# The four narrow maxima of an item ahead of its values

## The chip, the cores and the metric

The kernel runs on one core of a Trainium2 chip. The metric is device time in microseconds (us) of one launch, from the first to the last instruction of the program and what lies around them. Before the change it is 5533.32 us, the median of three runs (5531.68 to 5542.09).

## The reference

Eight samples of 256 channels x 32 x 32 in float32 go through four layers, each a kind of attention over the 1024 tokens of a sample. Cut to what matters here:

```python
# L0, L2: 8 heads of 32 channels        L1: the same 8 heads, and two more of 128 channels
xn = group_norm(x); q, k, v = split(qkv_w @ xn + qkv_b)
weight = softmax((q * s).T @ (k * s))          # [1024, 1024] for each sample and head
h = weight @ v                                  # then the projection, its bias and the residual
# L1 also: position added, a small 3x3 convolution whose sigmoid scales x, both attentions
#          concatenated, silu(... @ ff_w1) @ ff_w2 @ out_w, group norm, residual
# L3: one head of 256 channels
```

So each sample has three narrow attentions (8 heads of 32 channels; layers 0, 1 and 2) and two wide ones (two heads of 128 channels in layer 1, one of 256 in layer 3). The softmax subtracts the maximum of a row of scores. What is computed for that: an approximate score matrix once with tokens of q in partitions, whose row maxima are taken, and the exact scores a second time, transposed, with the negative maximum added inside the matmul as a 97th row.

## The kernel before, in words

**Samples and slots.** Attentions of two samples alternate: while one sample's attention runs, the work between two attentions of the other (projections, norms, convolution) is laid into its loop. `turns` makes these slots, `stages` gives each piece of between-work a place in units, and `plan` writes one list of events, PLAN, which every engine walks in the same order. Nothing is scheduled at run time: each engine executes its own instructions strictly in that order and waits on semaphores.

**Units, items, steps.** A narrow attention (kinds "0", "1", "2") has 128 units u. One unit is one score tile: 128 keys x 512 queries of one head. Four units, the four heads of a group at the same keys, are an item; 8 items are a step (one group of heads and one half of the queries), and there are 4 steps. In each unit PE issues `score`, then `rest` of the attention before (its tail), then `rest` of this one, then the between-work that is due.

**What a unit's pieces are.** ACT takes the exponential of each score tile into the ring PR of three items (L836). `values_narrow` (L562), at u = 6, 10, 14, ..., multiplies the probabilities of the item whose last score was u-3 with the values: eight matmul instructions in four column groups of 32, and their four results side by side in one bank, held over the step. `sums_narrow` (L577) does the same with ones, for the softmax's denominators: of the items 6 and 7 of a step directly (u % 32 = 2 and 4), and of the others after POOL has added their probabilities (L1133, L1120), at u % 32 = 6. `quad` (L626) is four approximate score matmuls of four heads for the *next* step, in four row groups of 32, one PSUM bank each; VectorE takes the row maxima of the four (L943), one in each of the units u to u+3. `quads_at` (L291) puts quads of steps 1 to 3 at every fourth unit from `first_quad` (L286), that is u = 2, 6, ..., 82; the first eight quads of an attention, and three of step 1, are issued by the between-work ahead of it. When all maxima of a step are there, `columns` turns them on PE, and a DMA lays them into the 97th row.

**Banks.** PSUM has 8 banks. `take` (L507) gives the bank that is not held and was given back longest ago, and makes PE wait until the engine that read its last content has read it. A score's bank goes to the back of that order at once; the banks of a quad are held and given back one per unit (`maximum`, `give`); the values' and the sums' banks are held for longer. In `quad` all four banks are taken, with their waits, before its first matmul.

In `rest` (L646), at a unit where both stand, PE therefore issues: the last part of the sums if due, the values, the first or second part of the sums if due, then the quad, then `maximum` (for a narrow attention it only gives a bank back).

Of the kernel before, what the change touches and what calls it, by code (L numbers as in the profile page):

```python
# [285 lines left out]
def first_quad(s):  # L286

    return 32 * (s - 1) - 4 * EARLY_QUADS + 2


def quads_at(att, u):  # L291

    if not att.wide:
        for s in range(1, att.steps):
            n, r = divmod(u - first_quad(s), 4)
            if r == 0 and 0 <= n < QUADS and (s > 1 or n >= EARLY_QUADS):
                return s, n
    return None


def maxima_at(att, u):

    out = []
    if u < att.units:
        for s in range(1, att.steps):
            first = 2 * (u - att.per * (s - 1)) if att.wide else u - first_quad(s)
            for p in range(first, first + (2 if att.wide else 1)):
                if 0 <= p < att.maxima and not (s == 1 and not att.wide and p < GROUP * EARLY_QUADS):
                    out.append((s, p))
    return out  # L310
# [14 lines left out]
def after_step(att, u, what):  # L325

    off = ((13, 14, 14, 15, 16) if att.wide else (38, 39, 40, 41, 43))[what]
    s, r = divmod(u - off, att.per)
    return s if r == 0 and 0 <= s < att.steps else None


def items_at(att, u):

    if att.wide:
        return [(s, kt) for s in range(att.steps) for kt in range(8) if u == att.per * s + max(4, kt + 3)]
    return [(s, i) for s in range(att.steps) for i in range(8) if u == att.per * s + 4 * i + 6]
# [21 lines left out]
def build_program(nc, x, pos, resident, stream, fold, out):  # L358
    ctx = ExitStack()
    with ctx:  # L360
# [115 lines left out]
        def until_read(eng, key):  # L476
            bank, n, _ = tiles[key]
            eng.wait_ge(read[bank], n + 1)
# [5 lines left out]
        def filling(key):  # L484
            return full[tiles[key][0]]

        def half(nh):
            return slice(nh * HALF, (nh + 1) * HALF)
# [11 lines left out]
        def _(pe):  # L500
            def mm(dst, lhsT, rhs, start, stop, **kw):
                return nc.tensor.matmul(dst, lhsT, rhs, start=start, stop=stop, **kw)  # L502
# [4 lines left out]
            def take(key, hold=False, says_full=True):  # L507

                bank = min((i for i in range(BANKS) if i not in held.values()), key=lambda i: (given[i], i))
                tiles[key] = bank, uses[bank], fulls[bank]  # L510
                if uses[bank]:
                    pe.wait_ge(read[bank], uses[bank])
                uses[bank] += 1
                fulls[bank] += says_full
                count["turn"] += 1
                given[bank] = count["turn"]
                if hold:
                    held[key] = bank
                return PS[bank]
# [33 lines left out]
            def sums(bank, probs, start, stop):  # L553
                for j in range(GROUP):
                    ins = mm(bank[D * j:D * j + D, :], ONES[:, 0:D], probs[:, j, :], start, stop,
                             tile_position=(0, D * j))
                return ins

            def narrow_probs(att, s, i):
                return PR[:, (att.item0 + 8 * s + i) % P_RING, :, :]  # L560
# [16 lines left out]
            def sums_narrow(att, s, part):  # L577
                key = ("sums", att.index, s)
                if part < 2:
                    if part == 0:  # L580
                        take(key, True)
                    sums(PS[tiles[key][0]], narrow_probs(att, s, ADDED + part), part == 0, False).then_inc(p_used, 1)
                else:
                    pe.wait_ge(p_added, att.adds0 + att.adds * (s + 1))
                    sums(PS[tiles[key][0]], ADD, False, True).then_inc(filling(key), 1)

            def values_wide(att, s, kt):
                until_read(pe, ("score", att.index, 8 * s + kt))
                keys = [("av", att.index, s), ("av2", att.index, s)][:att.ctiles]
                probs = PR[:, (att.item0 + 2 * s + kt // 4) % P_RING, kt % 4, :]  # L590
                for d, key in enumerate(keys):

                    if kt == 0:
                        take(key, True, d + 1 < att.ctiles)
                    col = (att.head(s) + d) * P
                    ins = mm(PS[tiles[key][0]][:, :], VT[:, att.index % 2, kt, col:col + P], probs, kt == 0, kt == 7)
                    if kt == 7 and d + 1 < att.ctiles:
                        ins.then_inc(filling(key), 1)
                if kt % 4 == 3:
                    ins.then_inc(p_used, 1)  # L600

            def sums_wide(att, s):
                key = ("sums", att.index, s)
                bank = take(key, True)
                pe.wait_ge(p_added, att.adds0 + att.adds * (s + 1))
                mm(bank[:, :], ONES[:, :], ADD[:, 0, :], True, True).then_inc(filling(key), 1)

            def maximum(att, s, p):
                key = ("max", att.index, s, p)
                if not att.wide:  # L610

                    give(key)
                    return
                bank = take(key)
                if s == 0 and p == 0:
                    until_read(pe, ("q", att.index, (1, 1)))
                    until_read(pe, ("k", att.index, (1, 1)))
                q, k = (wide_part(att.kind, o, "hi") for o in "qk")
                qt, kh = divmod(p, NH)
                q0 = s % NH * HALF + qt * P  # L620
                for ct in range(att.ctiles):
                    g = att.head(s) + ct
                    ins = mm(bank[:, :], q[:, g, q0:q0 + P], k[:, g, half(kh)], ct == 0, ct == att.ctiles - 1)
                ins.then_inc(filling(key), 1)

            def quad(att, s, n):  # L626
                g = s // NH
                if n == 0:
                    until_read(pe, ("k", att.index, (g, 1)))
                    until_read(pe, ("q", att.index, (g, s % NH)))  # L630
                qt, kh = divmod(n, NH)
                q0 = s % NH * HALF + qt * P
                keys = [("max", att.index, s, GROUP * n + j) for j in range(GROUP)]
                banks = [take(key, True) for key in keys]
                for j, key in enumerate(keys):
                    r = slice(D * j, D * j + D)
                    mm(banks[j][:, :], HIS[r, g, 0, q0:q0 + P], HIS[r, g, 1, half(kh)], True, True,
                       tile_position=(D * j, 0)).then_inc(filling(key), 1)
# [7 lines left out]
            def rest(att, u):  # L646
                if att.wide:
                    for s, p in maxima_at(att, u):
                        maximum(att, s, p)
                s = after_step(att, u, SUMMED)  # L650
                if s is not None and att.wide:
                    sums_wide(att, s)
                elif s is not None:
                    sums_narrow(att, s, 2)
                for s, i in items_at(att, u):
                    if att.wide:
                        values_wide(att, s, i)
                    else:
                        values_narrow(att, s, i)
                if not att.wide and u >= 34 and u % 32 in (2, 4) and u < att.units + 5:  # L660
                    sums_narrow(att, u // 32 - 1, (u % 32 - 2) // 2)
                four = quads_at(att, u)
                if four is not None:
                    quad(att, *four)
                if not att.wide:
                    for s, p in maxima_at(att, u):
                        maximum(att, s, p)
                s = columns_at(att, u)
                if s is not None:
                    columns(att, s)  # L670

                s = after_step(att, u, TURNED)
                if s is not None:
                    give(("sums", att.index, s))
                s = after_step(att, u, NORMED)
                if s is not None:
                    for name in ("av", "av2")[:att.ctiles]:
                        give((name, att.index, s))
# [46 lines left out]
            for event, it, i in PLAN:  # L725
# [74 lines left out]
                elif event == "v":  # L800
                    four, part = i
# [576 lines left out]
```

## Time and profile before

| | |
|---|---|
| median of three runs | 5533.32 us |
| profiled execution, its own time | 5545.02 us |
| its span, first to last instruction | 5543.2 us |
| mean granted TensorE clock | 0.933 |
| busy: PE matmul, PE weight load | 91%, 41% |
| busy: DVE, ACT, POOL | 51%, 50%, 58% |
| chain that ended last | PE 63%, DVE 9%, issue 9%, ACT 9%, POOL 8% |

PE is TensorE's matmuls, PEld its weight loads, DVE VectorE, ACT ScalarE, POOL GpSimd. A busy share is an average over stretches with different limits, and the chain of waits says which engine the end hung on, step by step. Instructions are named by the source line and by tile: out<-in. Nearly all matmuls are recorded under one helper line, L502, so the tile names tell them apart: `q_stack,k_stack` with 97 rows is a narrow score, `high_parts` with 32*128 a quad, `probs,v_tokens` with 128*32 narrow values, `probs,ones` and `probs_added,ones` sums.

### The profile page before, as it was taken

The page shows a single profiled execution, that of the slowest core. Times are in us where ns is not written, and L with a number is a line of the kernel's source. Part 1 is how long each engine was busy: PE and PEld are TensorE (multiplying, and loading weights), DVE is VectorE, ACT ScalarE, POOL GpSimd, SP SyncE. Part 2 cuts the span into 40 slices and gives each one's busy share as a digit, 9 for nine tenths or more (in the row PEclk, how much of TensorE's full clock was granted, in tenths as well). Part 3 has the DMA queues.
Part 4 walks back from the last instruction along what each step waited for, and adds up shares of the span by engine and source line. Part 5 has one row for each costly group of instructions (what it writes and reads, how often), then busy time and mean ns, then how long its engine had stood idle before and what let it go on. Part 6 is the DMA issues. An engine that isn't in the chain of part 4 may idle for free.

```text
span 5543.2 us, 63206 instructions
## 1 busy us (share of the span) xinstructions
PE 5032.5 (91%) x22016; PEld 2259.8 (41%) x22016; DVE 2851.5 (51%) x5110; ACT 2752.0 (50%) x4738; POOL 3232.3 (58%) x1777
## 2 busy tenths in 40 slices
PE   7788989999899998999999999999999999899887
PEld 3235333543335433354334543345333453334534
DVE  5345656256553565535655366544566346563362
ACT  3353665345663456524565255652556525555252
POOL 4474667546674476735767357664576636666363
PEclk8899889999899998999989999999899999899999
DMA  2112111022110211102210112101122012120020
GB/s 83 29 29 58 45 45 37 20 58 53 38 30 27 63 48 31 33 21 63 54 40 19 36 49 54 46 12 40 45 54 51 8 44 55 40 52 7 17 49 12
DMA packets 103609, 221.20 MB, mean 40 GB/s; under 512 B 31105, under 2 KB 33409, under 8 KB 103169
## 3 DMA queue, kind: packets, MB, share of 16 engines
q1 hardware_dynamic: 103296, 217.16, 15.1%
q8 instruction: 181, 2.97, 0.2%
q14 instruction: 132, 1.07, 0.1%
HBM read 56.47 MB, written 8.39 MB: 12 GB/s over the span
## 4 chain that ended last, share of the span: by engine, by line
PE 63%; DVE 9%; issue 9%; ACT 9%; POOL 8%; SPq 1%; DMA 1%; POOLq 0%; ACTq 0%; DVEq 0%
PE bank L502 63%; DVE max_cols L943 6%; POOL probs_added L1133 4%; ACT probs L836 3%; POOL probs_added L1120 3%; ACT L836 1%; ACT act L846 1%; DVE dev_squared L1054 1%; DVE stats L1040 1%; ACT act L855 1%; DVE sums_turned L965 1%; SPq L1220 0%; ACT L877 0%; SPq L1209 0%; DVE sums_turned L973 0%
## 5 line engine op out<-in xcount | busy, mean ns | idle before, releaser
L943 DVE TENSOR_REDUCE max_cols<-bank 128x1 f32<-128x512 f32 x3456 | 2183.8, 681 | 1822.3 <-PE bank L502 1818.5
L836 ACT ACTIVATE probs<-bank 128x512 f32<-128x512 f32 x3456 | 1921.2, 599 | 2267.2 <-PE bank L502 2131.4
L1133 POOL TENSOR_TENSOR probs_added<-probs_added,probs 128x1024 f32<-128x1024 f32 x768 | 1801.2, 2369 | 196.4 <-ACT probs L836 195.8
L502 PE MATMUL bank<-q_stack,k_stack 97*128 97x512 f32 (+1 forms) x3584 | 1669.6, 523 | 129.5 <-DVE max_cols L943 66.2
L502 PE MATMUL bank<-probs,v_tokens 128*32 128x512 f32 (+1 forms) x7168 | 1400.0, 649 | 44.1 <-ACT probs L836 44.1
L502 PEld LDWEIGHTS bank<-q_stack,k_stack 97*128 97x128 f32 (+1 forms) x3584 | 666.4, 197 | 891.5 <-issue 461.3
L502 PE MATMUL bank<-act,weight_stream 128*128 128x512 f32 x1792 | 952.8, 632 | 34.2 <-issue 8.3
L1133 POOL TENSOR_TENSOR probs_added<-probs 128x1024 f32<-128x1024 f32 x192 | 452.6, 2369 | 708.8 <-PE bank L502 682.1
L1120 POOL TENSOR_TENSOR probs_added<-probs 128x512 f32<-128x512 f32 x48 | 60.9, 1269 | 883.8 <-PE bank L502 851.9
L502 PE MATMUL bank<-high_parts 32*128 32x512 f32 x3072 | 409.6, 521 | 144.0 <-ACT probs L836 73.6
L502 PEld LDWEIGHTS bank<-probs,v_tokens 128*32 128x32 f32 (+1 forms) x7168 | 329.8, 123 | 515.2 <-issue 362.1
L502 PEld LDWEIGHTS bank<-high_parts 32*128 32x128 f32 x3072 | 160.3, 191 | 830.2 <-issue 752.2
L502 PEld LDWEIGHTS bank<-act,weight_stream 128*128 128x128 f32 x1792 | 327.8, 196 | 344.2 <-issue 278.2
L1120 POOL TENSOR_TENSOR probs_added<-probs_added,probs 128x512 f32<-128x512 f32 x288 | 373.0, 1295 | 57.5 <-ACT probs L836 32.0
L502 PE MATMUL bank<-k_stack 128*128 128x512 f32 x512 | 273.7, 573 | 53.0 <-ACT probs L836 36.2
L1172 POOL TENSOR_TENSOR low_parts<-full_parts,high_parts 128x512 fp32r<-128x512 f32 x192 | 243.9, 1274 | 100.0 <-ACT full_parts L909 100.0
L502 PE MATMUL bank<-weight_stream,act 128*128 128x256 f32 x1024 | 268.4, 391 | 0.0
L965 DVE STREAM_TRANSPOSE sums_turned<-bank 128x512 f32<-128x512 f32 x144 | 101.8, 707 | 321.1 <-PE bank L502 321.0
L502 PE MATMUL bank<-probs,ones 128*32 128x512 f32 x1536 | 225.1, 662 | 0.0
L502 PEld LDWEIGHTS bank<-weight_stream,act 128*128 128x128 f32 x1024 | 189.3, 192 | 71.1 <-issue 48.6
L955 DVE CAST neg_max_t<-bank 16x128 fp32r<-16x128 f32 (+1 forms) x144 | 39.7, 275 | 337.2 <-PE bank L644 337.2
L846 ACT ACTIVATE act<-act,gn_shift,gn_scale 128x512 f32<-128x512 f32 x192 | 148.3, 805 | 126.5 <-DVE gn_shift L1069 126.5
(82 smaller groups left out, 3479.5 us busy)
## 6 DMA issues: line engine op xcount, KB each, us to landing
k_stack<-high_parts SPq DMA_DIRECT2D x384, 128.0 KB, 2.4
q_stack<-high_parts SPq DMA_DIRECT2D x768, 64.0 KB, 2.0
weight_stream<-stream_dram SPq DMA_DIRECT2D x32, 768.0 KB, 4.4
k_stack<-low_parts SPq DMA_DIRECT2D x192, 128.0 KB, 2.4
q_stack<-low_parts SPq DMA_DIRECT2D x384, 64.0 KB, 2.0
act<-x_dram SPq DMA_DIRECT2D x8, 1024.0 KB, 6.5
act<-pos_dram SPq DMA_DIRECT2D x8, 1024.0 KB, 6.0
weight_stream<-stream_dram SPq DMA_DIRECT2D x16, 512.0 KB, 3.7
```

The lines of the kernel that those rows point to most:

```text
L502: return nc.tensor.matmul(dst, lhsT, rhs, start=start, stop=stop, **kw)
L836: act.activation(PR[:, m % P_RING, j, :], bank[:, :], ACT.Exp, scale=att.scale).then_inc(reading(key), 1)
L846: act.activation(act_buf(it.turn, dst)[:, t, half(nh)], act_buf(it.turn, src)[:, t, half(nh)], ACT.Identity, scale=GA[:, t:t + 1], bias=GS ...
L855: ins = act.activation(padded_image(it.turn)[D * j:D * j + D, 1 + rows * i:1 + rows * (i + 1), 2 - j:2 - j + SIDE], bank[D * j:D * j + D, ...
L943: dve.tensor_reduce(cols[:, kh, j, qt:qt + 1], bank[:, :], AX.X, ALU.max).then_inc(reading(key), 1)
L955: dve.tensor_copy(NT_[0:att.cols, :], bank[0:att.cols, 0:P]).then_inc(reading(key), 1)
L965: dve.transpose(RT[:, :], bank[:, :]).then_inc(reading(key), 1)
L1040: mark("stats", dve.bn_stats(ST[:, t, nh, :], act_buf(it.turn, src)[:, t, half(nh)]))
L1054: dve.tensor_tensor(SQ[:, :], DV[:, :], DV[:, :], ALU.mult).then_inc(gn_dev, 1)
L1120: pool.tensor_tensor(ADD[:, 0, :], one, two, ALU.add).then_inc(p_added, 1)
L1133: pool.tensor_tensor(ADD[:, js, :], one, two, ALU.add).then_inc(p_added, 1)
L1172: pool.tensor_tensor(low, whole, high.bitcast(F32), ALU.subtract).then_inc(lo_ready, 1)
```

## The change

In PE's `rest` the quad is issued ahead of the values (and ahead of the first and second part of the sums) instead of behind them. The `maximum` calls that give the banks back stay where they were, behind everything. No other engine's code changes. Since banks are handed out in PE's order, a quad that stands at a unit where values or sums take a bank now takes its four first.

```diff
@@ -652,6 +652,9 @@
                     sums_wide(att, s)
                 elif s is not None:
                     sums_narrow(att, s, 2)
+                four = quads_at(att, u)
+                if four is not None:
+                    quad(att, *four)
                 for s, i in items_at(att, u):
                     if att.wide:
                         values_wide(att, s, i)
@@ -659,9 +662,6 @@
                         values_narrow(att, s, i)
                 if not att.wide and u >= 34 and u % 32 in (2, 4) and u < att.units + 5:
                     sums_narrow(att, u // 32 - 1, (u % 32 - 2) // 2)
-                four = quads_at(att, u)
-                if four is not None:
-                    quad(att, *four)
                 if not att.wide:
                     for s, p in maxima_at(att, u):
                         maximum(att, s, p)
```

## Rows read from the trace of the kernel before

**Rows 1.** The page, busy us (share of the span) xinstructions:
```profile
PE 5032.5 (91%) x22016; PEld 2259.8 (41%) x22016; DVE 2851.5 (51%) x5110; ACT 2752.0 (50%) x4738; POOL 3232.3 (58%) x1777
```

**Rows 2.** Waits, whole span; engine waited <- releaser: us, times, longest us:
```profile
DVE max_cols L943 <- PE bank L502: 1818.5, 760, 27.7
...
PEld bank L502 <- ACT probs L836: 319.0, 523, 3.7
PEld bank L502 <- DVE max_cols L943: 311.4, 569, 3.8
...
PE bank L502 <- ACT probs L836: 205.0, 213, 4.1
...
PE bank L502 <- DVE max_cols L943: 142.1, 270, 3.3
...
PE bank L502 <- DVE mean_var L1045: 25.2, 12, 8.6
```

**Rows 3.** PE and PEld by shape: busy, mean ns | idle before <-releasers:
```profile
L502 PE MATMUL bank<-q_stack,k_stack 97*128 97x512 f32 x3072 | 1466.7, 544 | 129.5 <-DVE max_cols L943 66.2 <-ACT probs L836 34.4 <-DVE group_mean L1055 18.5
...
L502 PE MATMUL bank<-probs,v_tokens 128*32 128x512 f32 x6144 | 893.1, 656 | 44.1 <-ACT probs L836 44.1
...
L502 PE MATMUL bank<-high_parts 32*128 32x512 f32 x3072 | 409.6, 521 | 144.0 <-ACT probs L836 73.6 <-DVE max_cols L943 55.4 <-ACT full_parts L909 12.7
...
L502 PEld LDWEIGHTS bank<-q_stack,k_stack 97*128 97x128 f32 x3072 | 568.6, 198 | 847.0 <-issue 429.7 <-DVE max_cols L943 225.9 <-ACT probs L836 105.9
```

**Rows 4.** Windows: stretch: length, PE, PEld, DVE, ACT, POOL busy (x), PEclk, DMA, GB/s:
```profile
2897.50:3042.20 144.70, 136.20 (x693) 57.28 (x694) 79.66 (x141) 83.66 (x153) 104.78 (x50) 0.96 0.12 32
2551.60:2719.90 168.30, 154.18 (x714) 62.20 (x713) 101.47 (x181) 101.75 (x172) 116.76 (x60) 0.92 0.20 51
2719.90:2897.50 177.60, 160.03 (x729) 57.98 (x729) 102.35 (x185) 107.42 (x179) 115.42 (x60) 0.88 0.17 42
...
308.20:337.10 28.90, 26.77 (x161) 8.97 (x153) 22.06 (x38) 17.06 (x32) 23.38 (x10) 0.97 0.09 22
```

**Rows 5.** Timeline, laden turn at 2954 us; start, length, engine, line, op:
```profile
2954.09 0.82 PE L502 MATMUL bank<-q_stack,k_stack 97*128 97x512 f32 x2
2954.71 1.09 ACT L836 ACTIVATE probs<-bank 128x512 f32<-128x512 f32 x2 [0.42 <-PE bank L502]
...
2954.84 1.07 PE L502 MATMUL bank<-probs,v_tokens 128*32 128x512 f32 x8
...
2955.83 0.50 PE L502 MATMUL bank<-high_parts 32*128 32x512 f32 x4
...
2956.27 1.13 PE L502 MATMUL bank<-wv_wp,act 128*128 128x256 f32 x4
```

**Rows 6.** Timeline, the same attention's first and last moved turn:
```profile
2905.84 1.09 ACT L836 ACTIVATE probs<-bank 128x512 f32<-128x512 f32 x2 [1.63 <-PE bank L502]
...
2906.85 1.04 PE L502 MATMUL bank<-probs,v_tokens 128*32 128x512 f32 x8
...
2994.05 1.57 ACT L836 ACTIVATE probs<-bank 128x512 f32<-128x512 f32 x3 [0.71 <-PE bank L502]
...
2995.13 1.06 PE L502 MATMUL bank<-probs,v_tokens 128*32 128x512 f32 x8
```

**Rows 7.** Timeline, a score's weight load that waits for a maximum:
```profile
2909.10 0.19 PEld L502 LDWEIGHTS bank<-q_stack,k_stack 97*128 97x128 f32 x1 [0.66 <-DVE max_cols L943]
```

**Rows 8.** Timeline, a turn with nothing laid between, at 323 us:
```profile
323.79 0.51 PE L502 MATMUL bank<-high_parts 32*128 32x512 f32 x4
...
324.23 1.34 PE L502 MATMUL bank<-q_stack,k_stack 97*128 97x512 f32 x4
324.32 2.48 DVE L943 TENSOR_REDUCE max_cols<-bank 128x1 f32<-128x512 f32 x4 [0.23 <-PE bank L502]
324.77 2.07 ACT L836 ACTIVATE probs<-bank 128x512 f32<-128x512 f32 x4 [0.61 <-PE bank L502]
...
326.50 0.50 PE L502 MATMUL bank<-high_parts 32*128 32x512 f32 x4
```

## The prediction

> **What bounds the kernel now.** I read the shares first, then the waits, then the shapes on TensorE, then single turns. TensorE (PE) is busy for 91% of the span [rows 1]. The waits say that the other engines mostly wait for PE: the maxima on VectorE stood idle 1818 us for it. PE itself waited for the exponentials of ScalarE and for the maxima of VectorE, some hundreds of microseconds in four rows [rows 2]. So PE sets the pace; it is an in-order engine that stalls locally, and the change reorders exactly such a place. The shapes show what is reordered: 768 groups of four narrow maxima (a "quad") and 768 items of values [rows 3].
>
> Two kinds of stretch must be told apart. Of the 24 narrow attentions, 21 run beside another sample's projections and norms ("laden"): 145 to 178 us each. Three run with little beside them: the step of 28.9 us there has GpSimd busy 23.4 us, with additions for five of the eight items, so GpSimd's run and the turn to the next one set it [rows 4].
>
> **How many turns change.** Quads of steps 1 to 3 stand in the narrow loop at u = 2, 6, ... 82; that at u = 2 has no values beside it. That leaves 20 of an attention, 480 in all (420 laden, 60 not). The other 288 are issued by the between-work or at u = 2 and stay. DVE's, ACT's, POOL's and SP's orders are untouched, and no DMA moves. At u = 34 and 66 the quad is also moved past the first part of the sums; at u = 38 and 70 the last part stays ahead of it.
>
> **The engine's own time for the order.** A turn of now: two scores at 2954.09, values at 2954.84, quad at 2955.83, next work at 2956.27: values cost 0.99 us, the quad 0.44 [rows 5]. After: score, quad, values, score, the same pieces with the same number of changes between them. The pairs score-quad and quad-values are not in the trace. The nearest rows bound them: from the first of two scores to the values behind them it is 0.75 us, change and all, and a quad is left in 0.44 [rows 5]. I allow 0.1 us either way per turn, 480 x 0.1 = 48 us both ways, and take zero, except for u = 38 and 70, where sums and values no longer stand together: 48 turns x 0.1 = 5 us more.
> The trace shows values left only after 0.99 us although the quad, with a single pass, is left after 0.44 [rows 5]. The Trainium skill (TensorEngine Tiling (Array Packing), Key Properties) says that changing the tiling mode drains the engine. By that rule there are three drains in a turn before and after, four instead of three in the 48 turns named; by it the sum would gain the same few microseconds.
>
> **New stall ahead of the quad (the main term).** The quad takes four banks at once, the four free longest, and waits for the reader of each. By the rule of the banks (seven or fewer are free, each score and each given maximum goes to the back) the newest of the four was last used by the score one turn of the loop back (u-1) in about three of four quads, and by u-2 in the rest. The exponential of that score has not been taken when score u is issued. Now the values stand in between and hide it: at 2954.84 the values start; the two exponentials from 2954.71 take 1.09 us, so the first ends at 2955.26, and the quad, 0.2 later, could start at 2955.46. Now it starts at 2955.83 with no stall; after the change PE stands 2955.46 - 2954.84 = 0.62 us with the ready values queued behind it [rows 5]. In the first moved quad of that attention the first of the two exponentials from 2905.84 ended at 2906.39, before the values' 2906.85: nothing. In the last the exponentials end at 2995.62 and the values start at 2995.13: 0.63 us [rows 6]. The same subtraction, less whatever stall that turn has already, over all 20 turns of this attention (these are its first, its eleventh and its last) gives 0, 0.89, 0, 0.62, 1.00, 0.86, 0.41, 0.96, 0, 0, 0.61, 0, 0.95, 0.64, 0.86, 0.61, 0.51, 1.00, 0.62, 0.64: sum 11.2 us, 0.56 per turn. Bounds: 0, and 0.99 per turn (all the cover), 480 x 0.99 = 475 us. For 21 laden attentions: 21 x 11.2 = 235 us.
>
> Who is held up by the later values themselves? ACT, which needs their slot in the ring for the score at u+6, over an item later, and the sums behind them; neither is late by 1 us. The wait of a step's first quad for its q and k goes ahead of the values too (u = 22, 54), and those copies are long made.
>
> **What comes back.** First, where the newest bank waits for a maximum of the quad before, that maximum is itself earlier, since its own quad went ahead of its values: of the 11.2 us 2.6 vanish so. Second, scores now wait for banks whose maximum is not read, as 0.66 us at 2909.10 [rows 7], and for exponentials; with the quad up to a microsecond earlier relative to the scores, and ACT caught up during PE's stall, these shrink. Score waits in weight loads and matmuls sum to 226 + 106 + 66 + 34 = 432 us [rows 3]; the share of the moved turns is 480/768, 270 us, the upper bound (the lower is zero). Following each turn's own score waits I take 3.0 us of an attention, 63 for 21. Third, a delay that reaches a place where PE waits for a chain of a norm or of a projection's copy anyway is lost there; such waits are single rows of some 25 us [rows 2], and I take 40 us in all. Laden sum: 235 - 21 x 2.6 - 63 - 40 = 77 us.
> In the three lightly laden attentions the loop is another: quad 323.79, maxima from 324.32 for 2.48 us, next quad 326.50: VectorE's loop of 2.71 us [rows 8]. After, the loop goes quad 0.44, values 0.99, scores, the second or third exponential (1.6 to 2.1 us after the first score), 0.2: 3.2 to 3.7 us. But this falls in items that GpSimd's run mostly hides; what is left is about one turn per step, 9 x 0.6 = 5 us, and I take 8.
>
> Sum: 77 + 8 + 5 = 90 us. Profiled execution: 5545.0 us, of which span 5543.2; 5545 + 90 = 5635, 1.62% more. On the median of 5533.3: 5623; I say 5620.
>
> **Rivals.**
> (1) The early maxima win (faster). VectorE starts 0.4 to 1.0 us earlier, so scores no longer wait for its banks: 226 + 66 = 292 us of waits on maxima [rows 3], 5/8 of it 183; if the exponentials mostly are in time, so that the new stall is under some 0.2 us per turn, it is under 96 us and 5533 - 70 = about 5465 follows. For it: VectorE's idle time for PE, and turns as the first of rows 6. Against: rows 5 is the common turn. It decides when net new stall passes the score waits returned, about 0.25 us per turn.
> (2) Absorbed. If other waits take all that is added, as GpSimd does in the light steps [rows 4], the time stays within 11 us. Against: the laden steps wait little for GpSimd.
> (3) The clock gives a second price. The granted clock was 0.96 in the attention with the fewest stalls and 0.92 and 0.88 in the others, with PE's busy share 94, 92 and 90% [rows 4]: the lower level, 1.2 of 2.4 GHz, is granted more where PE stalls more. If the change costs 0.04 of the clock in 21 attentions with 150 us of busy PE each, that is 150 x 0.04/0.92 x 21 = 137 us on top of some 80: about 5750. The Trainium skill (TensorE: Matmul & The Clock Gate, section "A second HAM failure mode: psum-queue depth-cycling") says that short idles between groups of matmuls while PSUM banks are cycled make the clock oscillate; the rows here lean that way, but the laden attentions with long chains of a norm have the low clock too, so short stalls are not shown to be its cause.
> (4) That the edit does nothing is excluded: in 480 turns instructions of PE change places.
>
> **Numbers.** Forecast case 0.60 (its own range 5560 to 5690: the new stall between 0.4 and 0.75 us per turn, drains either way); clock 0.14; absorbed 0.07; faster 0.19. Faster and slower mean by over 0.2%, 11 us, about what a measurement of this kernel can tell from no change. The slower side is 0.60 + 0.14 = 0.74. The range 5500 to 5730 leaves out the better half of rival 1 and the far end of rival 3.
>
> **What would show it.** Right: the idle of PE before the quads' matmuls (144.0 us, of it 73.6 for exponentials [rows 3]) rises by 100 us or more and is now for the exponentials; values directly behind a quad with no wait of their own; maxima start nearer to the last score; score waits on maxima fall below 226 us; a common laden turn is longer by 0.3 to 0.6 us; the wide attentions keep their times. Wrong: if quads wait for nothing in most turns, the bank argument falls; if pairs score-quad and quad-values together cost 0.2 us more or less than 0.8, the drains do; if the clock moves by more than 0.01, rival 3 has a share.

## The result

The changed kernel takes 5667.0 us (median of 4 runs, 5663.7 to 5669.9) against 5537.7 us before on the same chip (4 runs): ratio 1.023, 95% interval 1.0214 to 1.0246, slower by some 127 us. The profiled execution's span is 5661.9 us, 118.7 us more than before, at a mean granted clock of 0.934 (before 0.933). Forecast were 5620 and a ratio of 1.016: the direction and the mechanism held; the slowdown is 1.4 times what was said (127 against 90 us).

The page of the kernel after, shares; PE is busy 41 us less in a span 119 us longer [rows 1]:

```profile
PE 4991.7 (88%) x22016; PEld 2265.0 (40%) x22016; DVE 2868.1 (51%) x5110; ACT 2745.9 (48%) x4738; POOL 3232.6 (57%) x1777
```

Its waits over the whole span, in the columns of [rows 2]:

```profile
DVE max_cols L943 <- PE bank L502: 1876.2, 762, 27.7
...
PEld bank L502 <- ACT probs L836: 443.5, 616, 3.7
PE bank L502 <- ACT probs L836: 401.5, 454, 5.1
...
PEld bank L502 <- DVE max_cols L943: 173.1, 291, 2.1
...
PE bank L502 <- DVE max_cols L943: 81.5, 114, 2.0
```

PE's waits for exponentials rose from 524 to 845 us, those for maxima fell from 454 to 255 us. A weight load and its matmul can show one wait twice, so these figures give directions and must not be added up.

PE (matmuls) and PEld (weight loads) by shape, answering to [rows 3]:

```profile
L502 PE MATMUL bank<-q_stack,k_stack 97*128 97x512 f32 x3072 | 1443.4, 541 | 84.9 <-ACT probs L836 37.5 <-DVE max_cols L943 26.9 <-DVE group_mean L1055 13.9
...
L502 PE MATMUL bank<-probs,v_tokens 128*32 128x512 f32 x6144 | 896.8, 658 | 34.4 <-ACT probs L836 34.4
...
L502 PE MATMUL bank<-high_parts 32*128 32x512 f32 x3072 | 411.0, 520 | 363.9 <-ACT probs L836 266.0 <-DVE max_cols L943 47.0 <-ACT full_parts L909 33.0
...
L502 PEld LDWEIGHTS bank<-q_stack,k_stack 97*128 97x128 f32 x3072 | 571.3, 200 | 954.9 <-issue 631.3 <-ACT probs L836 152.6 <-DVE max_cols L943 104.1
```

The quads are where the time went: PE's idle time before their matmuls rose from 144.0 to 363.9 us, and the part of it that an exponential ended rose from 73.6 to 266.0 us. The scores got something back: idle before their matmuls 129.5 -> 84.9, and their weight loads' waits for maxima 225.9 -> 104.1 us; but their waits for exponentials grew (105.9 -> 152.6).

The three kinds of laden attentions, in the columns of [rows 4]. The lines show the changed kernel: kind 0, kind 2, kind 1.

```profile
2607.20:2784.40 177.20, 157.39 (x714) 63.50 (x713) 100.56 (x181) 101.71 (x172) 116.71 (x60) 0.89 0.19 48
2784.40:2961.80 177.40, 152.12 (x729) 57.34 (x729) 103.26 (x185) 107.22 (x179) 115.50 (x60) 0.91 0.17 42
2961.80:3115.50 153.70, 139.60 (x692) 58.81 (x693) 80.46 (x141) 83.47 (x153) 104.85 (x50) 0.93 0.12 30
```

In these three, kind 0 went from 168.3 to 177.2 us, kind 2 from 177.6 to 177.4 and kind 1 from 144.7 to 153.7 (the last is the largest growth of its kind). Averaged over the seven of each, from the first exponential of an attention to that of the next, the growth is 10.0, 1.0 and 5.1 us; the three lightly laden ones grew by 7.7 us together, the wide ones shrank by 1.5 us together. All of it arises in steps 0 to 2; step 3, without moved quads, is the same within 0.4 us.

The turn of [rows 5], the eleventh moved one of that attention, in the changed kernel:

```profile
3018.02 0.81 PE L502 MATMUL bank<-q_stack,k_stack 97*128 97x512 f32 x2
3018.64 1.09 ACT L836 ACTIVATE probs<-bank 128x512 f32<-128x512 f32 x2 [0.42 <-PE bank L502]
...
3019.38 0.51 PE L502 MATMUL bank<-high_parts 32*128 32x512 f32 x4 [0.55 <-ACT probs L836]
...
3019.82 1.07 PE L502 MATMUL bank<-probs,v_tokens 128*32 128x512 f32 x8
```

Before, it was 0.75 us from the first of the two scores to the values, then 0.99 to the quad and 0.44 to the next work. Now it is 1.36 us from score to quad and 0.44 from there to the values. The quad waited until just after the first exponential ended (3018.64 + 0.55 = 3019.19, and 0.19 more), as was worked out for it. The new stall is 1.36 - 0.75 = 0.61 us.

### The profile page after: what moved, and what is told of

Its sections match the earlier page's. It is cut to its first block, busy times and chain, and to the rows that moved or that the text cites. A ratio compares the mean times of both kernels' runs of the same rounds, so it can differ in the third digit from the quotient of the medians.

```text
span 5661.9 us, 63206 instructions
## 1 busy us (share of the span) xinstructions
PE 4991.7 (88%) x22016; PEld 2265.0 (40%) x22016; DVE 2868.1 (51%) x5110; ACT 2745.9 (48%) x4738; POOL 3232.6 (57%) x1777
## 4 chain that ended last, share of the span: by engine, by line
PE 63%; ACT 12%; issue 9%; DVE 8%; POOL 6%; SPq 1%; DMA 1%; POOLq 0%; DVEq 0%; ACTq 0%
PE bank L502 63%; ACT probs L836 6%; DVE max_cols L943 4%; POOL probs_added L1120 3%; POOL probs_added L1133 3%; ACT L836 1%; DVE dev_squared L1054 1%; ACT act L846 1%; ACT full_parts L909 1%; ACT act L855 1%; ACT L877 1%; SPq L1220 0%; DVE stats L1040 0%; SPq L1209 0%; ACT high_parts L908 0%
## 5 line engine op out<-in xcount | busy, mean ns | idle before, releaser
L502 PE MATMUL bank<-q_stack,k_stack 97*128 97x512 f32 (+1 forms) x3584 | 1646.5, 520 | 84.9 <-ACT probs L836 37.5
L502 PE MATMUL bank<-high_parts 32*128 32x512 f32 x3072 | 411.0, 520 | 363.9 <-ACT probs L836 266.0
L502 PE MATMUL bank<-q_stack 128*128 128x512 f32 x512 | 203.9, 455 | 3.6 <-DMA neg_row<-neg_max_t 2.1
```

## The experiments

All are small edits to one of the two kernels. Times are medians, and each ratio is to the kernel before, measured beside that run. Its median moved between 5527.9 and 5541.9 us from one set of runs to the next, so small differences are read from ratios. The changed kernel's own time is 5667.0 us. Lines left out of an edit are marked " ...".

**1. Fill the stall.** If PE stands idle between score and quad, work put there is free. The filler is two matmuls of the shape of a score, 0.46 us in all, whose result is overwritten.

```diff
+            def filler(att, u, s, n):
+                key = ("max", att.index, s, GROUP * n)
+                bank, now = take(key, True), u // att.per
+                for _ in range(2):
+                    mm(bank[:, :], KS[0:97, GROUP * att.head(now), 0:P], QS[0:97, att.buf(now), 0, :], True, True)
 ...
                 four = quads_at(att, u)
+                if four is not None and u >= 6:
+                    filler(att, u, *four)
 ...
```

> The changed kernel with two idle score-like matmuls (0.46 us, result overwritten) into the quad's own oldest bank, after the score and ahead of the quad's other three waits, in all 480 moved turns: 221 us of added PE work. Theory (PE stands there anyway in 352 turns): most of it is swallowed by the stall, +40 to +110 us: 5705 to 5775. Rival (the loss is engine time of the order, not a wait): all is added, 5870 or more.

> The kernel before with the same two idle matmuls behind the score, ahead of the values. There the wait for the values' exponential swallows some 60 us of the 221: 5660 to 5740. Theory: the distance between the two kernels shrinks from 127 us to 0 to 80; rival: it stays 100 to 150.

Measured: the changed kernel with fillers took 5666.4 us, without them 5667.0: 480 fillers, 221 us of matmuls, added nothing. The kernel before with fillers took 5611.6 us against 5541.9, ratio 1.013 (1.0102 to 1.0158). The two filled kernels stand 55 us apart, the plain ones 125 to 129. Both times are below what was expected; the distance lies in the range of the theory. The quads' row by shape, of the changed kernel with fillers, then of the kernel before with fillers:

```profile
L502 PE MATMUL bank<-high_parts 32*128 32x512 f32 x3072 | 408.3, 517 | 134.3 <-ACT probs L844 36.8 <-DVE max_cols L951 31.1 <-issue 26.5
```

```profile
L502 PE MATMUL bank<-high_parts 32*128 32x512 f32 x3072 | 399.8, 509 | 52.6 <-DVE max_cols L951 25.1 <-ACT probs L844 18.5 <-ACT full_parts L917 7.2
```

The idle time before the quads falls by 230 us in the changed kernel (363.9 to 134.3), as much as was filled in, and by 91 us in the kernel before (144.0 to 52.6). So most of the loss is time in which PE stands between score and quad, not time that PE needs for another order. The run times alone would not show this, because the clock rose too, to 0.945 (changed, filled) and 0.955 (before, filled). An estimate: two runs of the kernel with short exponentials below, 5406.4 us at 0.941 and 5384.3 at 0.949, differ by 2.8 us for each 0.001 of the clock. By that the clock gave back some 30 and 60 us, and some 190 of the 221 us were hidden in the changed kernel, some 90 in the one before.

**2. Shorten what is waited for.** Each exponential is taken over a quarter of its columns; the other three quarters are left out of the computation.

```diff
-                act.activation(PR[:, m % P_RING, j, :], bank[:, :], ACT.Exp, scale=att.scale).then_inc(reading(key), 1)
+                act.activation(PR[:, m % P_RING, j, 0:P], bank[:, 0:P], ACT.Exp, scale=att.scale)\
+                   .then_inc(reading(key), 1)
 ...
```

> The kernel before, with each exponential taken over 128 of the 512 columns (the others hold ones and are left out of the computation). It is the base for the next run. PE waited 524 us for exponentials in all; some of it goes: 5250 to 5500.

> The changed kernel with the same short exponentials (three quarters of each left out). Theory (quads ahead of the values wait for the exponential of the score before last): that exponential is now there some 0.3 us sooner and ACT has no backlog, so the 127 us between the two kernels shrink to 30 to 80 us (what stays is the change from score to quad, 0.42 against 0.32 us, and part of the latency of PE and ACT). Rival (the order itself costs on PE): the distance stays 110 to 140 us.

Measured: 5385.9 and 5507.3 us, 121 us apart. The expectation of 30 to 80 was missed, and the rival's number of 110 to 140 was met. The changed kernel with short exponentials, by shape:

```profile
L502 PE MATMUL bank<-high_parts 32*128 32x512 f32 x3072 | 415.7, 526 | 288.1 <-ACT probs L837 141.3 <-DVE max_cols L945 102.3 <-ACT full_parts L911 22.6
```

and the kernel before with them:

```profile
L502 PE MATMUL bank<-high_parts 32*128 32x512 f32 x3072 | 411.3, 523 | 120.6 <-DVE max_cols L945 61.1 <-ACT probs L837 47.6 <-ACT full_parts L911 6.9
```

The rival's number need not have the rival's cause, because the stall before quads is still there: 288 against 121 us, 167 more, where the plain kernels differ by 220. Half of it is for exponentials, and more of it is for maxima than before (47.0 -> 102.3). An exponential of 278 ns instead of 599 (the mean of one) ends 0.3 us sooner, but the way from a score's matmul to the start of its exponential stays: 0.62 us in the turn above, 0.53 in the one below. The distance also holds a difference of the clock. The kernel before with short exponentials ran at 0.948 to 0.950 in three of its four runs, the changed one at 0.928 to 0.932, where the plain ones had 0.933 and 0.934. By the 2.8 us for each 0.001 this is some 47 of the 121 us, an estimate; the 74 that are left would lie in the expected range. So this pair of runs decides neither for the theory nor for the rival. In the light turns, where nothing else stands in the loop, the length of the exponential did count. There quads follow one another like this in the changed kernel:

```profile
322.59 0.51 PE L502 MATMUL bank<-high_parts 32*128 32x512 f32 x4 [0.20 <-ACT probs L836]
...
323.09 2.48 DVE L943 TENSOR_REDUCE max_cols<-bank 128x1 f32<-128x512 f32 x4 [0.22 <-PE bank L502]
324.02 1.19 PE L502 MATMUL bank<-q_stack,k_stack 97*128 97x512 f32 x4
324.55 2.07 ACT L836 ACTIVATE probs<-bank 128x512 f32<-128x512 f32 x4 [1.24 <-PE bank L502]
325.89 0.50 PE L502 MATMUL bank<-high_parts 32*128 32x512 f32 x4 [0.68 <-ACT probs L836]
```

It is 3.30 us from quad to quad, against 2.71 in [rows 8]. With short exponentials:

```profile
323.13 0.51 PE L502 MATMUL bank<-high_parts 32*128 32x512 f32 x4 [0.18 <-issue]
...
324.56 1.20 PE L502 MATMUL bank<-q_stack,k_stack 97*128 97x512 f32 x4
325.10 0.97 ACT L837 ACTIVATE probs<-bank 128x128 f32<-128x128 f32 x4 [1.84 <-PE bank L502]
325.93 0.50 PE L502 MATMUL bank<-high_parts 32*128 32x512 f32 x4 [0.18 <-issue]
```

It is 2.80 us.

**3. Other banks for the quad.** Of the free banks, the quad takes those of the three newest scores last.

```diff
-                bank = min((i for i in range(BANKS) if i not in held.values()), key=lambda i: (given[i], i))
+                late = issued[len(issued) - avoid:]
+                bank = min((i for i in range(BANKS) if i not in held.values()),
+                           key=lambda i: (owner[i] in late, given[i], i))
 ...
-                banks = [take(key, True) for key in keys]
+                banks = [take(key, True, avoid=3) for key in keys]
 ...
```

> The changed kernel, but a quad takes banks by another rule: of the free ones, those whose last user is one of the three newest scores come last. Theory (the quad, now ahead of the values, waits for exponentials that are not yet taken): the stall before the moved quads, 351 us by the trace, mostly goes, and the time falls from 5667 to between 5520 and 5590. Rival (the new order costs PE itself, by more drains between kinds of matmuls): no change, 5655 to 5675. Rival (a later values step starves others): no change either.

> The kernel before with the same rule of banks for quads. Theory: there the values hide most exponentials already; PE's idle for exponentials before all quads' matmuls was 74 us, so it gains 0 to 60 us: 5480 to 5535. Rival (order costs): 5530 to 5545. If scores now get the banks with exponentials still open, it could lose up to 20 us.

Measured: 5756.9 us (ratio 1.041) and 5605.4 (1.014), 90 and 77 us worse than without the rule and far outside what was expected. The changed kernel with it:

```profile
L502 PE MATMUL bank<-high_parts 32*128 32x512 f32 x3072 | 418.6, 530 | 463.3 <-DVE max_cols L949 178.5 <-ACT full_parts L915 86.9 <-ACT act L861 39.8
```

The exponentials no longer stand among the first three releasers, and the idle time is larger than in any other run. The banks that the quad takes instead had been released last by the maxima of the quad before, by the copies of q and k (`full_parts`), or by the work laid between. Of the two rules tried, oldest first is the better one. These runs refute "only the exponentials matter" and fit "four banks at once, and the newest reader is late"; they do not tell the two orders apart, since both kernels lost.

**4. Only the sums, and all but the turns that take a bank.**

```diff
 # one run, from the kernel before: the quad stands behind the values and ahead of the sums
-                if not att.wide and u >= 34 and u % 32 in (2, 4) and u < att.units + 5:
-                    sums_narrow(att, u // 32 - 1, (u % 32 - 2) // 2)
                 four = quads_at(att, u)
                 if four is not None:
                     quad(att, *four)
+                if not att.wide and u >= 34 and u % 32 in (2, 4) and u < att.units + 5:
+                    sums_narrow(att, u // 32 - 1, (u % 32 - 2) // 2)
 # the other, from the changed kernel: the old order at the four u named
+                ahead = u not in (34, 38, 66, 70)
 ...
```

> The kernel before, quad behind the values but ahead of the first part of the sums (u = 34 and 66 only, 48 turns). Theory: the values still stand in front and hide the wait, so 0 to +8 us: 5535 to 5550. Rival (the sums' and values' banks being taken after the quad's are what costs): a good part of the 127 us shows here, over 20 us.

> The changed kernel with the old order kept at u = 34, 38, 66 and 70, where the values or the sums take a bank: 384 of 480 turns stay moved, and the banks are handed out as before. Theory: 4/5 of the turns, at least 4/5 of the loss: 5630 to 5665. Rival (the other hand-out of banks is the cost): back to 5540 to 5570.

Measured: 5539.8 against 5527.9, ratio 1.0017 (1.0002 to 1.0032), and 5652.7, ratio 1.0224 (1.0201 to 1.0247). Both lie in the theory's range: moving the quad ahead of the sums costs at most 0.3%, and keeping the old order at the turns where banks change hands leaves the loss standing, so another hand-out of banks is not its main cause. By kind of laden attention the growth in the second run was 10.6, 3.3 and 1.2 us (kinds 0, 2 and 1), where the changed kernel had 10.0, 1.0 and 5.1: kind 1 gained from the old order at the four u, and kind 2 lost what experiment 6 is about.

**5. The quad a unit earlier or later.** `first_quad` shifts quads and their maxima together.

```diff
-    return 32 * (s - 1) - 4 * EARLY_QUADS + 2
+    return 32 * (s - 1) - 4 * EARLY_QUADS + 1      # the other run: + 3
```

> The kernel before with all quads and maxima of the narrow loop one unit earlier: score, quad, score, values, score. Theory: the values no longer stand between the newest scores and the quad, so the quad waits as in the changed kernel, though one score fewer stands before it: 5580 to 5680. Rival (only the direct exchange quad-values costs, or the drains): within 20 us of before.

> The kernel before with all quads and maxima of the narrow loop one unit later: score, values, score, quad, score. Theory: the values still stand behind the newest score whose bank the quad can need, so no loss: 5510 to 5560. Rival (quads lose by any place but the old one): 5580 or more.

Measured: earlier 5683.5 (ratio 1.028, 1.0256 to 1.0296), later 5573.2 (1.0072, 1.0047 to 1.0096), before 5531.8. Both lie above their ranges, earlier by 4 us and later by 13, though later does not reach its rival's 5580. The kernel with quads a unit earlier has the wait for exponentials, though quad and values did not change places within a unit:

```profile
L502 PE MATMUL bank<-high_parts 32*128 32x512 f32 x3072 | 410.5, 519 | 351.0 <-ACT probs L836 213.7 <-DVE max_cols L943 75.1 <-ACT full_parts L909 24.8
```

the one with quads a unit later has hardly more than before:

```profile
L502 PE MATMUL bank<-high_parts 32*128 32x512 f32 x3072 | 410.0, 520 | 170.6 <-ACT probs L836 76.6 <-DVE max_cols L943 40.3 <-DVE group_mean L1055 36.9
```

What both lose besides was not in the expectation: a score between quad and values makes four changes of the kind of matmul in a turn where there were three. A score that follows a score starts 0.22 us after it at the least, a quad 0.42 us; 480 x 0.2 us would be 96 us where nothing waits, which is a bound and more than the 41 us that the later quads lost. That is argued from the gaps and not tested by itself.

**6. Ahead only where it pays.** Item by item, the kind 2 attentions of the changed kernel stood 6.5 us ahead of those of the kernel before at u = 60 and had given it back by u = 84. In this run the quad goes ahead only there.

```diff
+                ahead = att.kind == "2" and u < 58
 ...
```

> Quads ahead of the values only in kind 2 attentions and only at u < 58 (13 turns of each, 104 in all), the old order elsewhere. In the changed kernel seven of these attentions stood 6.5 us each ahead of the old one by u = 60 and gave it back by u = 84. If what gave it back are the moved quads behind, 7 x 6.5 = 45 us are won: 5480 to 5505. If it is a fixed time of the norm chain that both reach, nothing is won: 5525 to 5545.

Measured: 5501.0 against 5541.9 us, ratio 0.9932 (0.9907 to 0.9957): faster than both kernels. Adding kind 1 at u = 6, 10, 14, 34 and 38:

> As c_mix, and in kind 1 attentions the quads of u = 6, 10, 14, 34 and 38 ahead of the values as well, where the changed kernel's items were shorter than before (by 1.1 us up to u = 16 and 1.3 at u = 32 to 40, seven attentions). If those gains stand by themselves, 7 to 17 us below c_mix: 5475 to 5495; if the next waits take them back, level with c_mix, 5495 to 5510.

Measured: 5511.1 against 5530.2, ratio 0.9966 (0.9950 to 0.9982): nothing on top; those gains are taken back.

What the first of the two won lies in the seven laden attentions of kind 2, which are 7.6 us shorter each; kinds 0 and 1 are within 0.6 us of before. Of the 7.6 us, 3.3 are there by u = 48 and 4.2 come from u = 52 to 56. Around u = 50 ACT changes its table twice, here in the timeline of the kernel before,

```profile
2782.74 1.28 ACT L855 ACT_TABLE_LOAD   x1
2784.03 2.07 ACT L855 ACTIVATE act<-bank,weights 32x512 f32<-32x512 f32 x3
2786.12 1.28 ACT L836 ACT_TABLE_LOAD   x1
2787.41 1.57 ACT L836 ACTIVATE probs<-bank 128x512 f32<-128x512 f32 x3
```

and a quad waits 3 to 5 us for an exponential, in every kernel without fillers that was looked at. The kernel before, windows ahead of that wait's end and behind it:

```profile
2776.00:2788.00 12.00, 6.64 (x33) 2.18 (x31) 7.28 (x14) 11.49 (x15) 6.96 (x3) 0.99 0.00 1
2788.00:2811.00 23.00, 22.36 (x53) 5.52 (x53) 6.01 (x14) 9.97 (x15) 10.06 (x5) 0.50 0.00 1
```

and the faster kernel at the same place:

```profile
2759.00:2771.00 12.00, 5.29 (x24) 1.90 (x22) 6.92 (x14) 11.57 (x15) 7.48 (x4) 0.87 0.00 0
2771.00:2794.00 23.00, 20.03 (x79) 5.91 (x80) 8.59 (x18) 16.13 (x23) 10.12 (x5) 0.87 0.01 1
```

Before, the granted clock stood at the lower level (1.2 of 2.4 GHz) for the whole of the 23 us behind the wait, with 53 matmuls; in the faster kernel 79 matmuls fit in the same time. The convolution's matmuls (`act,weights`) show it in the timeline, first before, then in the faster kernel:

```profile
2788.64 0.80 PE L502 MATMUL bank<-high_parts 32*128 32x512 f32 x4 [4.15 <-ACT probs L836]
2789.37 1.92 PE L502 MATMUL bank<-act,weights 96*32 96x512 f32 x2
```

```profile
2771.57 0.80 PE L502 MATMUL bank<-high_parts 32*128 32x512 f32 x4 [5.14 <-ACT probs L839]
2772.30 1.94 PE L502 MATMUL bank<-probs,v_tokens 128*32 128x512 f32 x8
2774.01 1.40 PE L502 MATMUL bank<-act,weights 96*32 96x512 f32 x2
2775.34 0.50 PE L502 MATMUL bank<-q_stack,k_stack 97*128 97x512 f32 x1
2775.77 1.05 PE L502 MATMUL bank<-act,weights 96*32 96x512 f32 x2
```

Both stand 4 to 5 us and both come out of it at the lower clock. In the faster kernel, with the values directly behind the quad, the full clock is back some 3 us later; in the one before not for over 20 us. It is tempting to say that the values bring it back, but the run of experiment 4 that kept the old order at four u refutes this. At u = 50 it too has the quad ahead of the values, and these are its timeline and its 23 us in one of the seven attentions:

```profile
4921.08 0.80 PE L502 MATMUL bank<-high_parts 32*128 32x512 f32 x4 [5.14 <-ACT probs L839]
4921.81 1.94 PE L502 MATMUL bank<-probs,v_tokens 128*32 128x512 f32 x8
4923.52 1.92 PE L502 MATMUL bank<-act,weights 96*32 96x512 f32 x2
```

```profile
4920.40:4943.40 23.00, 22.07 (x49) 5.83 (x49) 6.01 (x14) 8.43 (x14) 10.05 (x5) 0.50 0.00 1
```

The stand and the work behind it are the same as in the faster kernel, and the clock stays at the lower level. In six of the seven attentions of that run it stayed there for 16 to 26 us after the quad's start, in one for 4; in the faster kernel for 3 to 4 us in six and 17 in one; in the kernel before for 13 to 23 in all seven. What brings the clock back is not shown. That the time goes with it is: from u = 48 to 60, a kind 2 attention spent 19.7 us at the lower level and took 26.3 in the kernel before, 6.9 and 22.2 in the faster kernel, 5.2 and 21.7 in the changed one, and 21.2 and 27.4 in the run of experiment 4. So the gain of 41 us is read with care: it is a gain of the clock at least as much as of the quad's place, and it need not survive another edit.

## Why the prediction was right, and where its size was off

**The turns and the pieces.** As forecast, there are 480 turns, and values take 0.99 us and a quad 0.44 in either order. The pair quad-values takes 0.44 us, as a quad and a score did. The pair score-quad has a shortest gap of 0.42 us against 0.32 for score-values: 0.1 us more, the upper bound that was allowed and was taken as zero in the sum. The pairs score-quad and quad-values together cost 0.86 us, within 0.2 of the 0.8 that was named. From u = 6 to 85 the 21 laden attentions, 420 turns, grew by 118 us. To split this, each gap from the start of one group of matmuls to the start of the next was compared with the shortest gap of the same two kinds at the same level of the clock; what is over it is standing. The split leans on this choice of a base. Counted without regard to the clock, the rows of measured values would read 150, -38, -12, +18 and none for the clock.

| | forecast | measured |
|---|---|---|
| new stall ahead of quads, net of what went ahead of values | 180 | 207 |
| back from the waits of scores | -63 | -67 |
| lost in waits of the work laid between (forecast: norm chains) | -40 | -15 |
| the pieces' own time, sums included | 0 | +18 |
| the clock | 0 | -25 |
| sum | 77 | 118 |

The profile's own idle times, which count gaps over 0.15 us alone, stand nearer to the table: +201 us ahead of quads, -43 ahead of scores, -6 ahead of the work laid between, -3 ahead of values.

**The new stall, main term: right in kind, 27 us too small.** The turn that was worked out (0.62 us) measured 0.61. The order in which the kernel hands out banks gives the last user as was said: score u-1 in 347 of the 480 quads, u-2 in the other 133. PE stood idle over 0.15 us before 326 of the 480, against 122 before, and an exponential ended that wait in 262, against 62; the filler runs show that PE does stand there. The size was taken from one attention of kind 1 and multiplied by 21. Kind 1 measured 7.5 us net per attention, below the forecast's 8.6, but kinds 0 and 2 measured 10.6 and 11.6. The 0.1 us of the pair score-quad is in these figures, up to 2 us per attention, since the forecast's stall too was counted from where the values started.

**What comes back.** The scores returned 67 us, forecast 63. The third credit, 40 us lost in waits for norm chains that PE would have had anyway, came to 15. A chain of a norm begins with PE's own matmuls, so PE's delay moves its end as well; it is no fixed date that could swallow a delay. That is argued from the kernel's order and not tested. With 27 from the main term and 18 from the pieces this credit is why the sum was low.

**Luck.** By this count the clock gave 25 us back, a term that the sum did not have. Without it the miss would have been 66 us and not 41, so a part of the nearness of 5620 to 5667 is luck.

**The light attentions.** The loop was forecast at 3.2 to 3.7 us and measured 3.30 and 3.31. The loss was forecast at 8 us and measured 7.7, but not spread as said: the three changed by -0.5, +4.3 and +3.9 us, so the match of the sum is partly luck.

**The rivals.** Early maxima win: the scores' waits for maxima halved, but all that scores gave back is a third of the new stall. Absorbed: no. The second price by the clock was not paid: 0.933 and 0.934 over the span. It moved within it, though. In the mean of the seven attentions it fell from 0.919 to 0.901 in kind 0 and from 0.975 to 0.972 in kind 1, and rose from 0.896 to 0.919 in kind 2. That hid a loss: kind 2 came out level because it ran at a better clock around u = 50, where it gained 4.8 us each from u = 52 to 56. The rival had looked at the clock as a price only; here it was a gain.

**Signs named ahead.** Idle time before quads up by over 100 us: yes, 220. Waits of scores on maxima down: yes. A common laden turn longer by 0.3 to 0.6 us: not as a rule. The mean of the 420 turns is 0.28 us; in kind 1 the eight items from u = 52 to 80 grew by 0.6 to 1.4 us each, and those up to u = 48 on the whole by nothing. Wide attentions unchanged: yes. Values directly behind a quad with no wait of their own: yes, the standing ahead of values in these turns fell from 59 to 6 us. Clock moved by more than 0.01: no, by 0.001.

## What to carry to other kernels

Where an engine executes strictly in order, work that is ready is worth most directly ahead of an instruction that waits. Ask of each exchange which of the two waits, on whom, and how fresh that reader's work is, and bound the loss by the cover that is taken away. When a ring of buffers is shared, reading off who used the slot last gives the wait before anything is run. Count on another wait to swallow a delay only if that wait does not itself depend on the delayed engine. A filler of known size in the suspected gap is a quick test of whether the gap is idle, if the idle time before the next instruction is read beside the run time. And read the granted clock of every pair of runs before a difference of some tens of microseconds is given to the edit: here it moved by up to 0.017 between two kernels that differ in order alone.

## What the runs showed of the hardware

- 221 us of added matmuls cost 0 us in the changed kernel and some 70 us in the one before, and with them the mean granted clock was 0.945 instead of 0.934 and 0.955 instead of 0.933.
- After a stand of PE of 4 to 5 us the clock was at the lower level in all kernels without fillers that were looked at. It came back 3 to 4 us after the next matmul in some attentions and only after 13 to 26 us in others, and the same stand followed by the same matmuls did both (experiment 6).
- Some 200 us more of short stalls, 0.4 to 1 us each, left the mean granted clock where it was (0.933 and 0.934).
- In the changed kernel, four row-tiled matmuls (a quad) started 0.42 us at the least after a full-array score, and column-tiled ones (values) 0.32 us; whatever followed a quad started 0.43 us after it at the least.
